# Loads of the adjacency cells: one row quarter on 128 partitions per transfer, in place of one column quarter on 32 partitions

## The reference

```python
h = jnp.maximum(_layernorm(x, axis=-1), 0.0)
A_hat = adj + jnp.eye(adj.shape[0], dtype=adj.dtype)       # 8192 x 8192
d_inv_sqrt = jnp.sum(A_hat, axis=1) ** (-0.5)
A_norm = d_inv_sqrt[:, None] * A_hat * d_inv_sqrt[None, :]
out = x + jax.nn.relu(A_norm @ (h @ W.T))
```

## Time and profile before

| | us |
|---|---|
| median of 3 runs | 1196.89 |
| lowest and highest run | 1188.43, 1203.75 |
| the profiled execution | 1185.19 |
| its span, from the first instruction to the last | 1183.4 |

### The profile page before, as it was taken

The page is one execution under the profiler, slowest core; times in us unless marked ns, Lnnn a source line. Parts: engine busy times, 40 slices in busy tenths (PEclk is TensorE's granted clock), DMA queues, the critical chain, the costliest instruction groups (busy, mean ns, idle before and its releaser), DMA issues.

```text
span 1183.4 us, 9349 instructions
## 1 busy us (share of the span) xinstructions
PE 949.1 (80%) x2363; PEld 434.0 (37%) x2363; DVE 838.8 (71%) x1081; ACT 553.6 (47%) x1655; POOL 128.8 (11%) x102
## 2 busy tenths in 40 slices
PE   1713053483768879899998999999999999899997
PEld 1511021131323334344443444444444444344443
DVE  7952043373656867788887888888888888787785
ACT  0766675667655755462735626226246272100011
POOL 4021020110210101010101010000010000010011
PEclk9966576786979899999999999999999999999999
DMA  9999999999899999999999999999999799999993
GB/s 336 370 400 344 364 389 335 320 319 359 300 365 366 339 350 347 306 367 343 328 332 336 337 316 368 342 270 314 309 264 287 205 330 287 281 274 322 337 337 94
DMA packets 260486, 381.33 MB, mean 322 GB/s; under 512 B 10449, under 2 KB 237905, under 8 KB 260433
## 3 DMA queue, kind: packets, MB, share of 16 engines
q1 hardware_dynamic: 130288, 190.40, 51.3%
q10 hardware_dynamic: 130144, 190.34, 50.6%
HBM read 376.50 MB, written 4.19 MB: 322 GB/s over the span
## 4 chain that ended last, share of the span: by engine, by line
PE 43%; ACT 3%; DMA 3%; ACTq 1%; DVE 1%; SPq 1%; issue 0%; POOLq 0%; POOL 0%; DVEq 0%
PE bank L508 42%; DMA slot<-in_adj_dram 3%; ACT junk L547 2%; ACTq L289 1%; ACTq L297 1%; DVE adjT L701 0%; PE pre L484 0%; ACT slot L537 0%; ACT kept_cell L565 0%; SPq L342 0%; SPq L335 0%; DVE kept_cell L787 0%; POOLq L190 0%; POOL kept_cell L439 0%; SPq L289 0%
## 5 line engine op out<-in xcount | busy, mean ns | idle before, releaser
L508 PE MATMUL bank<-adjT,support 128*128 128x512 f32 x2048 | 908.2, 605 | 177.8 <-DVE adjT L701 177.7
L508 PEld LDWEIGHTS bank<-adjT,support 128*128 128x128 f32 x2048 | 394.4, 194 | 669.6 <-issue 666.4
L701 DVE STREAM_TRANSPOSE adjT<-slot 128x1024 f32<-128x1024 f32 x430 | 526.5, 1237 | 108.6 <-PE bank L508 97.2
L547 ACT ACTIVATE junk<-slot 128x384 bf16<-128x384 f32 (+2 forms) x732 | 348.1, 477 | 256.6 <-issue 144.9
L537 ACT ACTIVATE slot<-slot 128x6144 f32<-128x6144 f32 (+11 forms) x56 | 166.4, 2971 | 158.8 <-issue 74.7
L685 DVE TENSOR_REDUCE part<-slot 128x4 f32<-128x1536 f32 (+2 forms) x61 | 95.2, 1562 | 133.1 <-DMA slot<-in_adj_dram 133.1
L547 ACT ACTIVATION_READ_ACCUMULATOR junk<-slot 128x1 f32 x732 | 136.5, 186 | 0.0
L701 DVE STREAM_TRANSPOSE adjT<-kept_cell 128x1024 f32<-128x1024 f32 x70 | 85.0, 1231 | 27.6 <-PE bank L508 27.6
L428 POOL COPY kept_cell<-slot 128x2048 f32<-128x2048 f32 x35 | 65.1, 1892 | 352.5 <-DVE adjT L701 352.5
L565 ACT ACTIVATE kept_cell<-kept_cell,dinv 128x128 f32<-128x128 f32 x64 | 20.2, 389 | 176.1 <-DVE adjT L701 86.7
L416 POOL TENSOR_TENSOR dinv<-total,power 128x4 f32<-128x4 f32 x16 | 16.1, 1007 | 477.5 <-DVE total L755 477.5
(11 more groups left out here) (53 smaller groups left out, 166.3 us busy)
## 6 DMA issues: line engine op xcount, KB each, us to landing
slot<-in_adj_dram ACTq DMA_DIRECT2D x134, 768.0 KB, 13.3
slot<-in_adj_dram SPq DMA_DIRECT2D x134, 768.0 KB, 14.5
slot<-in_adj_dram ACTq DMA_DIRECT2D x66, 512.0 KB, 11.7
slot<-in_adj_dram SPq DMA_DIRECT2D x66, 512.0 KB, 12.6
slot<-in_adj_dram ACTq DMA_DIRECT2D x8, 1536.0 KB, 20.6
slot<-in_adj_dram SPq DMA_DIRECT2D x8, 1536.0 KB, 21.2
slot<-in_adj_dram SPq DMA_DIRECT2D x4, 1408.0 KB, 14.3
slot<-in_adj_dram ACTq DMA_DIRECT2D x4, 1408.0 KB, 15.0
```

The lines of the kernel that those rows point to most:

```text
L508: ins = nc.tensor.matmul(bank[bank_of(g)][:], support[:, v * R + t, :], adjT[at % TURNS][:, r, :], start=(n == first_of[g] and t == 0), st ...
L547: nc.scalar.activation(junk[at % JUNKS][:, :n], cells[:, c, :], ACT.Copy, accum_out=part[u % 2][:, k, c:c + 1]).then_inc(junk_done, 1)
L701: nc.vector.transpose(adjT[at % TURNS][:].rearrange("p t (c i) -> p t c i", i=Q), half.rearrange("p c (t r) -> p t c r", r=Q)).then_inc(t_ ...
```

## The change

The view of the matrix and the loop of `load_cells` change, and nothing else. In place of one transfer for each column quarter b, which fills 32 partitions with all 16 runs of each, there is one for each row quarter bb, which fills all 128 partitions with 4 of the 16 runs of each. The source pattern of a transfer was row (128), row quarter (4), column; it is now column quarter (4), row (128), column. The destination pattern was partition (32), run (16), column; it is now partition (128), run (4), column. Every element lands where it did, in runs of the same length; a transfer still moves 512 runs, a piece still takes 4 transfers, and each half of a piece is issued by the same queue as before.

```diff
-    adj_v = adj.rearrange("(bb u r) (b j) -> u b r bb j", bb=B, u=NB, b=B)
+    adj_v = adj.rearrange("(bb u r) (b j) -> u bb b r j", bb=B, u=NB, b=B)
...
         def load_cells(queue, quarters, m):
             kind, u, v, n = landing[m][:4]
-            for b in quarters:
-                queue.dma_start(piece(m)[b * Q:(b + 1) * Q, :, :],
-                                adj_v[u, b, :, :, v * CELL:(v + n) * CELL]).then_inc(ld_slot[slot_of[m]], 16)
+            rows = piece(m).rearrange("p (c bb) j -> p bb c j", bb=B)
+            for bb in quarters:
+                queue.dma_start(rows[:, bb, :, :],
+                                adj_v[u, bb, :, :, v * CELL:(v + n) * CELL]).then_inc(ld_slot[slot_of[m]], 16)
```

## The result

The changed kernel takes 3158.4 us (median of 4 runs, 3150.84 to 3164.74) against 1195.38 us before: 2.641 times as long, 95% interval 2.623 to 2.660. The forecast was 3400 us with a range of 2870 to 4400.

What follows compares the result with a forecast made beforehand. Before, transfers bound the first half and TensorE the second; changed, four DMA engines carry all cells. 3304 us of work on the busiest engines + 27 at the ends + 70 for dry queues = 3400 us, range 2870 to 4400.

Steps and rivals of the forecast that it cites:

- The mechanism: Transfers of cells: source's outermost count of 4 deals each to the same four of 16 DMA engines; chance 0.74 near own rate.
- three cells: 65 x 512 = 33,280 runs x 66.8 ns: Loads of three-cell pieces: a quarter of their runs on each of four engines, 2223 us.
- its two neighbours: Loads of two-cell pieces, 15,872 runs x 48.1 ns = 763 us, and one-cell pieces, 1536 x 29.4 = 45 us.
- the bound at 26.1 GB/s: Lower bound: all 74.9 MB an engine at 26.1 GB/s, without the 10.7 ns a run, 2870 us.
- the other two lines: Far pieces on 16 engines, 228 us, and the remaining bytes, mostly in runs of 512 bytes, 45 us.
- Moments when the queues run dry: Allowance of 2% (70 us) for times when the queues of the four engines are empty.
- Cover: Long transfers hide slower TensorE clock and blocked issues, costing nothing; without it at most ScalarE's own 554 us.
- The crowding rival: Four engines filling neighbouring partitions in step get in each other's way: 5600 us, chance 0.16.
- the one-queue stretch with 212 GB/s: Before the change, 924 to 928 us: one queue's packets, 16 engines in 64 partitions, 13.3 GB/s an engine; evidence for crowding.
- Over 16 engines: Rival: transfers of cells dealt out by partitions over 16 engines, faster, about 1115 us, chance 0.05.
- engines in turn: Rival: each transfer of cells uses four engines, but others in turn; no change, about 1185 us, chance 0.05.
- Signs: If right: DMA share 0.25 to 0.35, about 115 GB/s, about 5700 small packets, median issue to landing above 50 us.

Runs made afterwards that it cites:

- pairs: Changed kernel with each transfer of cells cut in two, so the source's outermost count is 2 in place of 4; 5900.0 us (one run).
- again: Only the pieces loaded again for the last stage are loaded as changed, all others as before the change; 1566.0 us (one run).
- micro: No computation, zeros stored; ten stages each load pieces in another transfer form, runs of 1536 bytes; outermost counts 2, 4, 8 gave 50, 99, 200 GB/s.
- same_half: Kernel before the change, but SP loads column quarters 0 and 2, ScalarE's queue 1 and 3, so both fill the same 64 partitions; 1531.7 us (one run).
- places: No computation; two engines of 32 partitions each at partitions 0 to 63, 32 to 95, 64 to 127, runs of 1536, then 6144 bytes; no kernel time given.

## Why the prediction was right

- **The count of small packets.** The reading that 10,449 packets are 16 for each of 653 transfers held to one packet: 5696 after the change, 29,456 with sixteen transfers a piece, 5697 in "pairs", 9344 in "again" ((396 - 92 + 257) x 16 + 92 x 4). This was the step that turned a question about the chip into one that the page answers.
- **The mechanism.** Right: four engines, and "pairs", "again" and the stages of "micro" with counts of 2, 4 and 8 each give 25 GB/s an engine. The times of the two kernels are those that the bytes of the busiest engine say. The rule of the Trainium skill that decided it (DMA: Bandwidth & Descriptors, on why a DMA increments its semaphore by 16) held here for counts of 2, 4, 8 and 16.
- **The term that was mis-sized** is "three cells: 65 x 512 = 33,280 runs x 66.8 ns", with its two neighbours. At four engines the runs take 61.4, 42.2 and 23.5 ns: 2043 + 670 + 36 = 2749 us in place of 3031. The text took the rate of 16 engines for four, by the nearest row, and gave the other end as the bound at 26.1 GB/s; the truth lay between. That bound is not quite what its text says: 26.1 GB/s is the rate of rows of 6144 bytes with the 10.7 ns in it, and 0.0365 ns a byte alone would be 27.4 GB/s and 2730 us. With the 273 us of the other two lines the work is 3022 us.
- **Moments when the queues run dry.** 70 us were allowed. The profiled run is 3164.7 us; 3022 + 27 leaves 116. The share does not fall below 0.26 in stretches of 20 us between 20 and 3140 us, so dry spells are not the reason. The stretches with far pieces and cells together are: from 75 to 90 us 221 GB/s move at a share of 1.04, and in the packets of the trace runs of 1536 bytes take some 135 ns there and rows of 6144 bytes some 440, about twice their usual 65 and 240. Over the whole run the packets of cells with 1536 and 1024 bytes take 68.1 and 47.2 ns in the mean, against 65.4 and 46.1 where cells alone move; over a quarter of all of them that is 107 us for each of the four engines, an estimate of the same size as the 116. The sum had priced far pieces and cells as if each ran undisturbed beside the other. So it was 282 us too high in the runs and 46 too low in this term, and part of the closeness of 3400 to 3158 is that the two cancel.
- **Cover.** Right: ScalarE's issues stretched to 11 us and TensorE's clock fell, and next to nothing of either shows in the time.
- **The rivals.** The crowding rival is real as a mechanism (same_half, places) but not at work where the changed kernel moves cells alone: with 1536-byte runs four engines reach 100 GB/s, as much each as two or eight. Where far pieces and cells meet, a share of 1.04 with 221 GB/s looks like the crowded stages of "micro"; whether it is the place in the partitions that they meet at was not tried. Its row, the one-queue stretch with 212 GB/s, was read rightly as crowding: one queue alone has 211 in "micro" with 32 partitions a transfer and 373 with 128, and two queues in one half have 260. The Trainium skill (SBUF — State Buffer, on the DMA port swizzle) gives partitions 32 apart within a half one port; 41 against 53 GB/s in "places" agrees. "Over 16 engines" and "engines in turn" fall with the packets and the share.
- **Signs.** A share of 0.27 where cells alone move, 0.35 over the span, and 121 GB/s over the span came as named. The median from issue to landing, said to rise above 50 us, cannot be read, since the profile gives none for these transfers; the one landing on the chain, the last, came 26 us after its issue.

## What to carry to other kernels

Before reshaping a transfer, look at the outermost count of both of its patterns, the one in memory and the one on the chip: counts of 2, 4 and 8 left fourteen, twelve and eight of the 16 engines idle here, however wide the transfer was on the chip's side. The count of packets under 512 bytes, by the number of transfers, tells how many engines each one used (as long as no run of data is that short), and a DMA share of a quarter beside a kernel that waits for transfers says the same. When two queues load one buffer in transfers of 32 partitions, let each keep its own half of the partitions: the same transfers in another order cost 28% here (same_half, one run).

## What the runs showed that was not expected

- Sixteen engines that write into one half of the partitions move 260 GB/s from two queues and 211 from one, at a DMA share of 1.09 and 1.10. A share near 1 is no sign that the engines are at their rate. It passes 1 with one queue alone as well, so that packets of both queues on one engine are not the only reason for it.
- What a run costs beside its bytes was 4.5 ns at four engines, columns outermost, and 9.3 at sixteen, rows outermost. Which of the two differences does it is open.
- Cells on four engines and far pieces on sixteen slow each other: about twice the time for a run of either from 75 to 90 us of the changed kernel.
- A walk with columns outermost is slower with sixteen engines, 316 against 373 GB/s with the same runs on 128 partitions, while counts of 2, 4 and 8 keep 25 GB/s an engine.
- Long runs are not always faster: 6144 bytes gave four engines some 80 to 89 GB/s, where 3072 gave 103. Two of the four engines write into each half, and "places" shows such a pair at 39 to 43 GB/s in place of 53.
